# Cross-attention with FFN on one core: every event of a row placed anew, FFN weight products one row ahead

## The reference

```python
qh = split(layernorm(x) @ Wq.T + bq) / 4
kh = split(ctx @ Wk.T + bk)
vh = split(ctx @ Wv.T + bv)
attn = softmax(qh @ kh.T)
x = x + (attn @ vh) @ Wo.T + bo
h1 = layernorm(x) @ W1[g].T + b1[g]
x = x + h1 @ W2[g].T + b2[g]
```

## Time and profile before

| | |
|---|---|
| median of three runs | 577.42 us (576.56, 577.42, 577.71) |
| profiled execution, span from first to last instruction | 574.6 us |
| the same execution's time outside the span | not recorded; the median less the span is 2.8 us |
| lead, to the first exp | 41.0 us |
| eight rows of 64 exps | 41.0 to 551.2 us |
| end | 23.4 us |
| mean granted clock of TensorE | 0.964 |

### The profile page before, as it was taken

The page is one execution under the profiler, slowest core; times in us unless marked ns, Lnnn a source line. Parts: engine busy times, 40 slices in busy tenths (PEclk is TensorE's granted clock), DMA queues, the critical chain, the costliest instruction groups (busy, mean ns, idle before and its releaser), DMA issues.

```text
span 574.6 us, 13508 instructions
## 1 busy us (share of the span) xinstructions
PE 547.0 (95%) x4353; PEld 342.1 (60%) x4353; DVE 455.2 (79%) x841; ACT 381.5 (66%) x703; POOL 274.4 (48%) x319
## 2 busy tenths in 40 slices
PE   7899999999999999999999999999999999988997
PEld 6646555656566556656566556656566656443576
DVE  5895987898869987898879997898878997876134
ACT  4324767776767777786767776776767776768731
POOL 5251194324961478324961478324961175214711
PEclk9856999999999999999899999999899999999999
DMA  6675433447244654447144654447242624322201
GB/s 206 145 184 183 130 94 76 131 113 239 70 131 135 188 150 113 129 112 238 62 132 129 161 181 111 129 112 238 63 135 66 203 58 114 94 94 74 95 0 38
DMA packets 46704, 72.67 MB, mean 126 GB/s; under 512 B 12162, under 2 KB 22730, under 8 KB 46666
## 3 DMA queue, kind: packets, MB, share of 16 engines
q1 hardware_dynamic: 46666, 72.18, 44.7%
HBM read 41.99 MB, written 4.47 MB: 81 GB/s over the span
## 4 chain that ended last, share of the span: by engine, by line
PE 50%; DMA 15%; POOL 11%; issue 10%; DVE 8%; SPq 2%; ACT 2%; POOLq 0%; DVEq 0%; ACTq 0%
PE pv L535 12%; PE st L521 10%; PE misc L709 9%; PE nat L510 7%; DMA inv_sum<-inv_dram 5%; DVE neg_max L1040 4%; PE misc L595 4%; DMA ln_bc<-ln_dram 3%; PE misc L585 3%; DMA inv_dram<-inv_small 2%; POOL xT_in L1314 2%; DMA ln_dram<-norm_in 2%; POOL norm_in L1277 2%; POOL pair_ctx L1298 2%; SPq L402 2%
## 5 line engine op out<-in xcount | busy, mean ns | idle before, releaser
L1040 DVE TENSOR_REDUCE neg_max<-nat 128x1 f32<-128x512 f32 x504 | 329.9, 684 | 76.4 <-PE nat L510 72.4
L878 ACT ACTIVATE probs<-st 128x512 f32<-128x512 f32 x502 | 283.8, 599 | 109.4 <-PE st L521 105.6
L510 PE MATMUL nat<-ks,qs 63*128 63x512 f32 x504 | 225.8, 477 | 4.1 <-DVE neg_max L1040 2.3
L521 PE MATMUL st<-qs,ks 64*128 64x512 f32 x502 | 211.1, 458 | 13.3 <-ACT probs L878 10.7
L521 PEld LDWEIGHTS st<-qs,ks 64*128 64x128 f32 x502 | 89.4, 188 | 108.6 <-ACT probs L878 90.3
L535 PE MATMUL pv<-probs,vs 128*32 128x512 f32 x1024 | 139.8, 619 | 0.6 <-ACT probs L878 0.5
L510 PEld LDWEIGHTS nat<-ks,qs 63*128 63x128 f32 x504 | 93.8, 191 | 22.4 <-DVE neg_max L1040 17.5
L709 PE MATMUL misc<-w_in 64*128 64x256 f32 x512 | 69.2, 381 | 0.0
L1298 POOL TENSOR_TENSOR pair_ctx<-pair_ctx,inv_sum 128x512 f32<-128x512 f32 x15 | 19.1, 1275 | 99.3 <-DMA inv_sum<-inv_dram 99.3
L709 PEld LDWEIGHTS misc<-w_in 64*128 64x128 f32 x512 | 52.7, 186 | 11.1 <-issue 8.8
L535 PEld LDWEIGHTS pv<-probs,vs 128*32 128x32 f32 x1024 | 20.5, 108 | 38.8 <-issue 34.4
(11 more groups left out here) (204 smaller groups left out, 1006.0 us busy)
## 6 DMA issues: line engine op xcount, KB each, us to landing
ks<-hi SPq DMA_DIRECT2D x64, 128.0 KB, 2.8
qs<-hi SPq DMA_DIRECT2D x64, 128.0 KB, 2.6
w_in<-w SPq DMA_DIRECT2D x16, 512.0 KB
w_in<-w2T SPq DMA_DIRECT2D x16, 512.0 KB
x_in<-x SPq DMA_DIRECT2D x8, 512.0 KB, 3.3
ctx_in<-ctxT SPq DMA_DIRECT2D x8, 512.0 KB, 3.3
ks<-lo SPq DMA_DIRECT2D x32, 128.0 KB, 2.8
qs<-lo SPq DMA_DIRECT2D x32, 128.0 KB, 2.5
```

What stands on the lines that cost most here:

```text
L510: mm((nat_of(n) if bank is None else bank)[:, :], qs[own, 2 * g + jj, c * P:(c + 1) * P], ks[own, 2 * g + jj, :], start=True, stop=True).t ...
L521: mm(st_of(u, prep)[:, :], ks[rows(jp), 2 * g + jj, kc * P:(kc + 1) * P], qs[rows(jp), 2 * g + jj, :], start=True, stop=True).then_inc(st_ ...
L878: act.activation(probs[kc % 2][:, j, :], st_of(u, prep)[:, :], ACT.Exp).then_inc(exp_done, 1)
L1040: dve.tensor_reduce(neg_max[:, g % 2, at:at + 1], (nat_of(n) if bank is None else bank)[:, :], AX.X, ALU.max, negate=True).then_inc(max_do ...
```

## The change

Five things are changed together.

1. The tables of units have other numbers, and some events that stood together have places of their own now (`pv`, the four parts of `normalise`, the statistics).
2. The FFN product of a row is computed a row earlier: turn b computes that of row b+1, the product of row 0 stands in the lead between the first `nat` blocks, and row 7's turn has none. Its results have two buffers (hence the `odd` argument and a loop over pairs of rows). The loads of W1 and W2 and `b2_parts` move with it.
3. `stack_quad`, six DMAs that spread keys and queries of a quad, is split into `stack_keys` and `stack_queries`, three each, and SP's list has another order.
4. POOL's list has another order: both `inverse_root`s stand ahead of `x_norm`, `ctx_rest` ahead of `attn_rest`.
5. In the lead, the activation table is loaded by a first small exp, the context is split before any weights, each weight waits only for its own load, and SP issues the weights of row 0's FFN ahead of the first copies of keys and queries. `x_split(1)` moves into unit 5 of turn 0.

The diff, cut to its core:

```diff
-W21_UNITS = (51, 51, 52, 52, 52, 53, 55, 55, 59, 59, 60, 63, 63, 63, 63, 66)
+W21_UNITS = (48, 48, 51, 52, 53, 54, 59, 59, 63, 63, 65, 66, 66, 68, 68, 68)
-PV_AT = 1
+PV_UNITS = (7, 11, 15, 19, 25, 25, 29, 33, 39, 40, 47, 50, 55, 57, 61, 64)
-Z_UNITS = (43, 43, 43, 43, 47, 47, 47, 48)
+Z_UNITS = (41, 42, 43, 43, 45, 45, 45, 45)
-ODD_AT = (35, 1)
+ODD_AT = (37, 0)
-JOIN_AT = (37, 2)
+JOIN_AT = (61, 4)
-HI_AT = (8, 13, 17, 20)
+HI_AT = (13, 13, 18, 21)
-ATTN_AT = (51, 15)
+ATTN_AT = (63, 17)
-NORM_AT = 33
+NORM_AT = (32, 33, 33, 34)
-X_SPLIT_AT = 47
+X_SPLIT_AT = 59
+FIRST_X_SPLIT_AT = 5
+AGGR_AT = (15, 28)
-INVERT_AT = (43, 7)
+INVERT_AT = (45, 5)
-OUT_AT = (49, 53)
+OUT_AT = (45, 48)
+FIRST_W21_AT = (3, 4, 5, 6, 7, 8, 9, 10, 11, 12, 13, 14, 15, 16, 19, 20)
...
-        b2_all = sb("b2_all", [P, D])
+        b2_all = [sb(f"b2_all{i}", [P, D]) for i in range(2)]
-        w21_hi = sb("w21_hi", [P, F, D], F32R)
+        w21_hi = [sb(f"w21_hi{i}", [P, F, D], F32R) for i in range(2)]
-        w21_lo = sb("w21_lo", [P, F, D], F32R)
+        w21_lo = [sb(f"w21_lo{i}", [P, F, D], F32R) for i in range(2)]
...
-            def turn(b, post, prep, load):
-                if post:
-                    stack_quad(b, 3)
-                    gather_sums(b - 1, 1)
+            def turn(b, odd, post, prep, load):
                 if load:
                     load_x(b + 2)
                 if post:
+                    gather_sums(b - 1, 1)
+                    stack_queries(b, 3)
                     save_inverse(b - 1, 1)
-                store_max(b, 1)
+                if prep:
+                    load_ffn(b + 1, 0)
+                    load_ffn(b + 1, 1)
                 if post:
                     spread_inverse(b - 1, 1)
                 if load:
-                    load_xT(b + 2)
+                    load_ctx(b + 2)
+                store_max(b, 1)
                 if prep:
-                    stack_quad(b + 1, 0)
+                    load_bias(b + 1)
+                if post:
+                    stack_keys(b, 3)
+                if prep:
+                    stack_keys(b + 1, 0)
+                    stack_queries(b + 1, 0)
+                store_max(b, 2)
                 if load:
                     save_ln(b + 2)
                     spread_ln(b + 2)
-                if post:
-                    load_ffn(b, 0)
-                store_max(b, 2)
-                if post:
-                    load_ffn(b, 1)
-                    load_bias(b)
+                    load_xT(b + 2)
+                gather_sums(b, 0)
                 if prep:
-                    stack_quad(b + 1, 1)
-                gather_sums(b, 0)
-                if load:
-                    load_ctx(b + 2)
-                save_inverse(b, 0)
+                    stack_queries(b + 1, 1)
                 store_max(b, 3)
-                spread_inverse(b, 0)
                 if prep:
-                    stack_quad(b + 1, 2)
+                    stack_keys(b + 1, 1)
                 if post:
                     store_out(b - 1, 0)
                     store_out(b - 1, 1)
                 if prep:
+                    stack_keys(b + 1, 2)
+                save_inverse(b, 0)
+                if prep:
+                    stack_queries(b + 1, 2)
+                spread_inverse(b, 0)
+                load_y(b)
+                if prep:
                     store_max(b + 1, 0)
-                load_y(b)
...
-            load_w(WK, wkT, const_qk)
-            sp.dma_start(bqk[:, 1, :], bk).then_inc(const_qk, 16)
-            load_w(WQ, wqT, const_qk)
-            sp.dma_start(bq_in[:, :], bq).then_inc(const_qk, 16)
+            load_w(WK, wkT, const_k)
+            sp.dma_start(bqk[:, 1, :], bk).then_inc(const_k, 16)
+            load_w(WQ, wqT, const_q)
+            sp.dma_start(bq_in[:, :], bq).then_inc(const_q, 16)
             load_w(WV, wvT, const_in)
             sp.dma_start(bv_all[:, 0, :], bv.partition_broadcast(P)).then_inc(const_in, 16)
             sp.dma_start(bo_all[:, :], bo.partition_broadcast(P)).then_inc(const_in, 16)
             load_w(WO, woT, const_in)
+            load_ffn(0, 0)
+            load_ffn(0, 1)
+            load_bias(0)
             load_xT(1)
             sp.wait_ge(dve_set, 3)
             sp.dma_start(ks[KN:P:HALF, :, :].bitcast(F32), ones[0:64, :]).then_inc(ones_in, 16)
@@ -475,13 +500,18 @@
                 if g == 3:
...
-                stack_quad(0, g, FIRST_ORDER)
+                stack_keys(0, g, FIRST_ORDER)
+                if g == 0:
+                    sp.wait_ge(hi_ready, FIRST_ORDER.index((0, 0)) + 1)
+                    spread_slot(qs, 0, g, 0)
+                    spread_slot(qs, 0, g, 2)
+                    sp.wait_ge(lo_ready, FIRST_ORDER.index((0, 0)) + 1)
+                    spread_slot(qs, 0, g, 1)
+                else:
+                    stack_queries(0, g, FIRST_ORDER)
                 if g == 1:
                     save_ln(1)
                     spread_ln(1)
-            load_ffn(0, 0)
-            load_ffn(0, 1)
-            load_bias(0)
...
-            def w21_begin(b, post, prep):
-                wait(pe, ffn_loaded, 96 * (b + 1))
+            def w21_begin(b, post):
+                wait(pe, ffn_loaded, 96 * (b + 2))
                 wait(pe, max_ready, 4 * b + 4)
-                if prep:
-                    wait(pe, lo_ready, 4 * (b + 1) + 3)
-                    wait(pe, v_ready, 2 * (b + 1) + 2)
+                wait(pe, lo_ready, 4 * (b + 1) + 3)
+                wait(pe, v_ready, 2 * (b + 1) + 2)
...
-                for n, at in enumerate(W21_UNITS if prep else LAST_W21_UNITS):
-                    if at == u:
+                        z_step(b - 1, 1 - odd, n)
+                for n, at in enumerate(W21_UNITS):
+                    if prep and at == u:
                         if n == 0:
-                            w21_begin(b, post, prep)
-                        w21_step(b, n, prep)
+                            w21_begin(b, post)
+                        w21_step(b + 1, n, load)
...
-                    if u % 4 == PV_AT:
-                        if u > 4:
-                            pv(b, u // 4 - 1)
-                        elif post:
-                            pv(b - 1, 15)
-                    jobs(b, u, post, prep)
+                    for n, at in enumerate(PV_UNITS):
+                        if post and at == UNITS + u:
+                            pv(b - 1, n)
+                    for n, at in enumerate(PV_UNITS):
+                        if at == u:
+                            pv(b, n)
...
+                for k, at in enumerate(FIRST_W21_AT):
+                    if at == n:
+                        if k == 0:
+                            pe.wait_ge(ffn_loaded, 96)
+                        w21_step(0, k, True)
...
             act.wait_ge(dve_set, 2)
-            act.wait_ge(const_qk, CONSTS_QK)
+            act.activation(even_ctx[:, 0:P], ones[:, :], ACT.Exp)
+            ctx_split(0)
+            act.wait_ge(const_k, CONSTS_QK)
             act.activation(w_hi[:, WK], w_in[:, WK], ACT.Copy).then_inc(w_hi_ready, 1)
-            ctx_split(0)
+            act.wait_ge(const_q, CONSTS_QK)
             act.activation(w_hi[:, WQ], w_in[:, WQ], ACT.Copy, scale=SCALE).then_inc(w_hi_ready, 1)
             act.activation(bqk[:, 0, :], bq_in[:, :], ACT.Copy, scale=SCALE).then_inc(act_set, 1)
-            normalise(0, 0, x_in, 0, C)
+            act.wait_ge(rstd_ready[0], 1)
+            normalise(0, x_in, 0, C)
             act.wait_ge(act_set, 1)
             first_hi_half(0)
             for f in range(F):
                 first_xT_copy(f)
             first_hi_half(1)
+            first_hi_half(2)
             act.wait_ge(const_in, CONSTS)
             act.activation(w_hi[:, WV], w_in[:, WV], ACT.Copy).then_inc(w_hi_ready, 1)
-            first_hi_half(2)
             act.activation(w_hi[:, WO], w_in[:, WO], ACT.Copy).then_inc(w_hi_ready, 1)
             first_hi_half(3)
             act.wait_ge(dve_set, 5)
             act.wait_ge(w_ready, 4)
             act.wait_ge(qk_first, 4)
-            x_split(1)
             ctx_split(1)
             turns(act, turn)
-            for f in range(F):
-                w21_copy(LAST, f)
             attn_split(LAST, 1)
...
-            def turn(b, post, prep, load):
+            def turn(b, odd, post, prep, load):
                 if post:
-                    v_stack(b, 3)
                     divide(b - 1, 1)
-                    attn_rest(b - 1, 1)
                 if load:
                     inverse_root(0, b + 2)
+                if post:
+                    attn_rest(b - 1, 1)
+                    inverse_root(1, b - 1)
+                    v_stack(b, 3)
+                if load:
                     x_norm(b + 2)
                 if post:
-                    inverse_root(1, b - 1)
-                    add_b2(b - 1)
-                b2_parts(b)
+                    add_b2(b - 1, 1 - odd)
+                if prep:
```

(27 more changed lines are left out.)

251 lines of the change are left out of this document (135 added, 116 removed).

## The result

The changed kernel takes 614.41 us (median of 4 runs, 608.76 to 614.77) against 577.57 us before: a ratio of 1.062, interval 1.056 to 1.069. It is 6.2% slower. The prediction said 567.5 us, a gain, and had 582 as its upper end: it had the wrong sign. The profiled execution took 614.77 us with a span of 612.8, 38.2 us over the span of before.

A forecast was written before the change was run, and what follows sets the result against it. It took the engines' waits for each other, no engine filling the row, as the bound. Span: 574.6 - 22.6 - 3.8 - 3.0 + 19.2 + 0.5 = 564.9; plus 2.8 gives 567.7, given as 567.5 us, range 549 to 582.

The forecast's parts named there:

- SP's order in a row: the new wait: Unit 16: the maxima land late behind the FFN weights; 3.5 us in rows 1 to 5, 1.7 in row 6, 19.2 together.
- Rival 1: Unit 16: the maxima land before the row reaches it, so no wait; 548.5 us, chance 0.24.
- Rival 2: The wait at unit 16 halves the clock in six rows; new term 29.8 us, time 578.3 to 586.8, chance 0.20.
- the sign that the prediction named for it: Granted clock 0.50 once a row behind unit 16.
- ACT's waits and the clock: Steady rows: ACT's waits for POOL's division and root go, 22.6 us; three half-clock stretches go, 3.8 us.
- rival 3: Old waits re-met elsewhere, half of 22.6 us back; 559.8 before the queue's term, 570 to 579 with it; chance 0.13.
- 0.8 of the waits recovered: Share of ACT's 28.3 us of waits taken as gained, 22.6 us; between 0.5 and 1.0.
- The clock's 1.27 us a stretch: Gain for each of three half-clock stretches after units 33 to 36, 3.8 us in all, between 0 and 4.6.
- The lead: Before row 0: earlier table load against later root, maxima and x_norm(1); +0.5 us in sum, between -5 and +5.
- Row 7: The last row loses its 64 FFN matmuls; 3.0 us gained, at most 3.5.

## Why the prediction was wrong

The step that failed is the term "SP's order in a row: the new wait". The prediction named its place (unit 16 of rows 1 to 6) and its cause (the maxima behind the weights in one queue), and both are what happened. Its size was 19.2 us in the sum and 47.2 in the runs, a factor of 2.5, and this alone changes the sign: 577.4 - 22.6 - 3.8 - 3.0 + 47.2 + 0.5 = 595.7. Rival 1, that there is no wait, is refuted. Term by term, in profiled spans; rows 1 to 6 of two kernels that differ in nothing there were 1.1 us apart (376.8 and 375.7), so a term read from two profiles is good to about that:

- **The new wait behind the weights: forecast +19.2, measured +47.2.** This is rows 1 to 6 of the change (424.0 us) less those of the kernel with the weights behind stack_keys (376.8). 36.2 us of it are there by exp 16; the other 11.0 come behind it, nearly all in units 16 to 19. Four steps were mis-sized. The reciprocal, moved from unit 7 to 5, ended 6.6 to 8.0 us into a row (forecast 5.3; before the change 7.5), so the save of the inverse stood at 6.9 to 8.3 (5.5). SP issued the weights 1.2 to 1.9 us after it, and their packets started 9.3 to 11.2 us in (7.9). The last of them moved at 17.0 to 20.0 (14.9). The maxima moved another 1.4 to 4.3 us later, and in row 3 PE had them 0.9 us after that, 21.1 us in (18.2). Each step is a bit late, and all add up, because each waits for the one before. The Trainium skill's sentence on ring order ("DMA: Bandwidth & Descriptors", section Queues, rings and completion order), which the prediction cites, agrees with the trace: in row 3 the maxima were issued at 12.1 us and moved at 19.8, behind the last of the weights at 17.0.
- **Rival 2, the halved clock:** right as a companion, and the sign that the prediction named for it is there. The changed kernel shows ten stretches at granted clock 0.50 between 71.6 and 573 us, 54.6 us in all, and one of them runs past exp 16 in each of rows 1 to 6, for 2.2 to 5.2 us behind it, 22.7 us together. The 11.0 us behind exp 16 stand there. With the weights moved and the rows written out there are 3.4 us of it between 69 and 506 us. The cost of 4.8 us a row, from which the rival said that the whole change loses, was passed at exp 16 already: 6.0 us a row, and 7.9 with what follows. But the rival's time, 578 to 587, missed too, as it had the same 4 us of wait. A window of such a stretch, behind exp 16 of row 1 (at 132.79), with PEclk third from the end:

```profile
133.20:136.40 3.20, 3.20 (x18) 1.98 (x20) 2.51 (x5) 2.35 (x5) 1.98 (x4) 0.50 0.05 16
```

- **ACT's waits and the clock: forecast -26.4, measured -17.0**, from rows 1 to 6 of the kernel without the queue's wait and without the loop (368.7 us, before 385.6). The waits themselves are gone. But units 0 to 14 take 16.0 us in the changed kernel against 13.4 before, and units 33, 37, 43 and 51 are shorter by 0.9 to 2.0 us each. Something in the new places and orders, which I priced at 0, made the first units longer; no run isolates which. Exp 16 of an undisturbed row comes at 16.8, not at the 14.5 that I had. So rival 3 holds a part: 0.8 of the waits recovered was too much. The clock's 1.27 us a stretch also does not follow from the 1.5 less 0.4 beside it; that is 0.5 us of the sum.
- **The loop: not in the forecast, measured +8.1** in rows 1 to 6 of the profiles (376.8 less 368.7; 7.0 between the two kernels that differ in the loop alone), 5.4 of it at the passage from row 3 to row 4; 4.5 us in the medians. The diff shows the body of two rows, and I took it as nothing but a renaming of buffers.
- **The lead: forecast +0.5, measured +4.65** to exp 0. I had load_ctx(1) late, but had not seen that ACT's split of it stands ahead of exp 0 in the program; the first maxima stood behind it too. The edit of that one load brings exp 0 back to 41.35, and row 0 gives half of that back. Row 0, forecast as no change, was 1.8 us shorter in the change. The FFN product did hide: from 30.6 to 44.2 us the granted clock is 1.0, where it was 0.50 before.
- **Row 7: forecast -3.0, measured -2.9**, and that the two agree is luck. Row 7 of the change had 6.8 us at granted clock 0.50. With the weights behind stack_keys, the same row ran at full clock and took 53.3 us, 5.7 less than before, but the end behind it took 27.4 us instead of 23.4.

47.2 - 17.0 + 8.1 + 4.65 - 1.8 - 2.9 = 38.25, against the 38.2 of the spans. Rows 1 to 6 add up by construction, as their terms are differences along one line of kernels.

What stays open: why row 2 of the change lost 8.6 us by exp 16 and row 3 only 5.2, with the same instructions (in row 2 the weights were issued 1.0 us later, their last packet moved 2.1 us later and the maxima 3.6 us later than in row 3); and how the 47.2 us divide between the order in the queue and the shared DMA engines, since moving the weights to ACT's queue also moved them in time.

## What to carry to other kernels

In these runs a large load delayed every small transfer behind it in the same queue. List all of these with the units at which they are due, not only the first: moving the load past one made the next pay 7 us. When such a chain of steps decides the sign, read each step's place from the row as it will be (here the reciprocal, its save, the issue, the first packet) and put the late end in the sum, not the early one: here the errors along the chain did not cancel. And a unit that has become longer is no loss in itself; look whether the sum of the row moved.

## What was not expected of the hardware

- A jump back to the head of a loop whose body is two of these rows kept PE idle for 3.25 us and DVE for 3.46. ACT ran one split in that time and no exp; POOL, which had work left, went on. Meanwhile 8 and 16 KB packets of no transfer of the kernel moved (8 packets, 0.07 MB, on an instruction queue from 285 to 300 us). Half clock followed, for 6.8 us in the run with the weights behind stack_keys. Written out, the same stretch with its 56 matmuls took 6.81 instead of 12.19 us. The loop of one row before showed nothing of the kind: 1.7 to 1.9 us from exp 63 to the next exp 0 at every passage. That the engines waited for their code is not shown; the packets only suggest it.
- The 2.1 MB of weights of row 3 did not move at one rate: 250 GB/s for the first 4.5 us, then 389 from 266 to 268 us. The first half of the bytes took 4.3 us, the second 3.4.
- With the DMA engines full in both, 2 KB packets moved at 269 GB/s (269.6 to 272.4 us, DMA share 1.05) and 4 KB packets at 389 (266 to 268 us, 1.01).
